# Multi-query attention: where the row maxima join the stacked queries

## The reference, cut to what matters

```
q = (x @ Wq + bq).reshape(Bx, Tx, HEADS, HD)
k = (x @ Wk + bk)[:, :, None, :]
att = jnp.einsum('bthd,bThd->bhtT', q, k) / math.sqrt(HD)
att = jnp.where(causal, -jnp.inf, att)
att = jax.nn.softmax(att, axis=-1)
```

## Time and profile before

| | us |
|---|---|
| median of 3 runs | 1833.64 (1832.84 to 1834.93) |
| the profiled execution, whole | 1835.51 |
| its span from first to last instruction | 1833.4 |

### The profile page before, as it was taken

How to read it: one execution, slowest core, us unless ns; L and a number is a source line. 1 busy time by engine, 2 the same in 40 slices (tenths; PEclk the granted TensorE clock), 3 DMA queues, 4 the chain that set the end, 5 groups by cost and what they waited for, 6 DMA issues and landing times. The chain is left out here.

```text
span 1833.4 us, 25467 instructions
## 1 busy us (share of the span) xinstructions
PE 1655.7 (90%) x7232; PEld 1261.5 (69%) x7232; DVE 1175.8 (64%) x1999; ACT 1196.7 (65%) x2231; POOL 1274.3 (70%) x1025
## 2 busy tenths in 40 slices
PE   3688989889898979898699999997999999999998
PEld 2355766767676757686366666664788888888887
DVE  5668677686959586564466666662556665665655
ACT  2236575756575655676277787885677777777776
POOL 3568597777878676667177777776567676767765
PEclk8788999999999999999699999998899999999999
DMA  3012222122121222332000000000233333333331
GB/s 116 1 46 58 64 62 65 59 62 71 57 71 58 69 58 75 94 98 63 1 1 1 1 2 0 1 1 18 75 94 102 98 93 103 98 98 96 100 93 52
DMA packets 115177, 108.96 MB, mean 59 GB/s; under 512 B 7003, under 2 KB 81888, under 8 KB 115040
## 3 DMA queue, kind: packets, MB, share of 16 engines
q1 hardware_dynamic: 115040, 107.39, 19.8%
HBM read 105.27 MB, written 2.10 MB: 59 GB/s over the span
## 5 line engine op out<-in xcount | busy, mean ns | idle before, releaser
L465 POOL TENSOR_TENSOR ARENA_R<-ARENA,ARENA_R 128x512 fp32r<-128x512 f32 x384 | 573.6, 1495 | 330.5 <-ACT ARENA_R L460 328.9
L557 DVE TENSOR_TENSOR ARENA<-ARENA,pair 128x512 f32<-128x512 f32 x512 | 350.0, 684 | 415.8 <-PE pair L340 330.4
L517 ACT ACTIVATE ARENA<-bank 128x512 f32<-128x512 f32 x512 | 305.0, 596 | 319.9 <-PE bank L340 319.2
L338 PE MATMUL pair<-ARENA_R 128*128 128x512 f32 x1064 | 423.2, 398 | 44.4 <-ACT ARENA L918 19.1
L339 PE MATMUL pair<-ARENA_R 128*128 128x512 f32 x1064 | 417.7, 393 | 0.0
L340 PE MATMUL pair<-ARENA_R 128*128 128x512 f32 x1064 | 417.4, 392 | 0.0
L527 ACT ACTIVATE ARENA_R<-ARENA 128x512 fp32r<-128x512 f32 x512 | 319.6, 624 | 57.8 <-DVE ARENA L557 57.4
L533 DVE TENSOR_TENSOR ARENA_R<-ARENA,ARENA_R 128x512 fp32r<-128x512 f32 x384 | 313.7, 817 | 0.0
L842 POOL TENSOR_TENSOR ARENA_R<-ARENA,ARENA_R 128x512 fp32r<-128x512 f32 x192 | 249.5, 1313 | 79.9 <-ACT ARENA L1026 76.4
L338 PEld LDWEIGHTS pair<-ARENA_R 128*128 128x128 f32 x1064 | 202.8, 191 | 104.0 <-ACT ARENA L918 22.5
L338 PE MATMUL bank<-ARENA_R 128*128 128x512 f32 x568 | 242.4, 427 | 19.2 <-DVE ARENA L1502 14.4
(11 more groups left out here) (213 smaller groups left out, 2252.4 us busy)
## 6 DMA issues: line engine op xcount, KB each, us to landing
ARENA<-in_L_ffn_Wg_dram SPq DMA_DIRECT2D x128, 256.0 KB, 2.6
ARENA<-in_L_ffn_Wu_dram SPq DMA_DIRECT2D x128, 256.0 KB, 2.6
ARENA<-in_L_ffn_Wd_dram SPq DMA_DIRECT2D x128, 256.0 KB, 2.8
X<-in_L_attn_a_x_dram SPq DMA_DIRECT2D x8, 256.0 KB, 5.7
out_dram<-X SPq DMA_DIRECT2D x8, 256.0 KB, 3.2
CST<-in_tables_dram SPq DMA_DIRECT2D x1, 835.5 KB, 5.0
ARENA<-in_tables_dram SPq DMA_DIRECT2D x1, 768.0 KB, 5.2
CST<-in_tables_dram SPq DMA_DIRECT2D x1, 256.0 KB, 4.9
```

The costliest lines, as they stand in the source:

```text
L338: pe.matmul(dst, wh, xh, start=start, stop=False)
L465: g.tensor_tensor(WL[:, x % 2, part, :], WS[:, x % 2, part, :], WH[:, x % 2, part, :].bitcast(F32), ALU.subtract).then_inc(F.wl, 1)
L517: act.activation(SG[:, c % 2, :], bank[c % 2], ACT.Silu).then_inc(F.sil, 1)
L557: v.tensor_tensor(HF[:, c % FC, :], SG[:, c % 2, :], bank[2 + c % 2], ALU.mult).then_inc(F.mul, 1)
```

## The change

The identity product of `stack2` goes: the two products with the maxima now start and end the group in PSUM by themselves. ScalarE's two copies go. VectorE gets `add_maxima`: for h = 0 and 1, one tensor_tensor that adds the stacked queries (from SBUF) to the bank (from PSUM) and writes Q2. It stands in VectorE's slot behind maximum k = 1. Waits that guarded QST by `q2_ready` now name `q2_used`, as VectorE reads QST.

```
@@ ScalarE
-                    if k == T_LAG - 1 and live(t, b, 1):
-                        o, ob = n - 1, 1 - b
-                        for h in range(2):
-                            act.wait_ge(B.q2_ready, 2 * o + h + 1)
-                            after(act, B.t_ready, UNITS * o)
-                            act.activation(Q2[:, 2 * h:2 * h + 2, :],
-                                           r3(bank[6 + h], 2), ACT.Copy).then_inc(B.q2_used, 1)
-                    after(act, B.q2_ready, 4 * (nxt.n - 1))
+                    after(act, B.q2_used, 4 * (nxt.n - 1))
@@ TensorE, stack2
-                    pe.matmul(dst, SELR[:, SID, :], QST[:, p, j, ob * SEQ:(ob + 1) * SEQ], start=True, stop=False)
                     for a in range(2):
                         m = pe.matmul(dst[:, a * P:(a + 1) * P], NMP[:, a, j, :], SELR[:, SID, :],
-                                      start=False, stop=(a == 1))
+                                      start=True, stop=True)
@@ VectorE
+            def add_maxima(o, p, ob):
+                for h in range(2):
+                    js = slice(2 * h, 2 * h + 2)
+                    v.wait_ge(B.q2_ready, 2 * o + h + 1)
+                    after(v, B.t_ready, UNITS * o)
+                    v.tensor_tensor(Q2[:, js, :], QST[:, p, js, ob * SEQ:(ob + 1) * SEQ].bitcast(F32),
+                                    r3(bank[6 + h], 2), ALU.add).then_inc(B.q2_used, 1)
...
                     if t.real():
                         maximum(t, b, k)
+                    if k == T_LAG - 1 and live(t, b, 1):
+                        add_maxima(n - 1, t.p if b == 1 else 1 - t.p, 1 - b)
```

More of the change, by code:

```diff
@@ L1009, in slot @@
                         if closing(t, b, k, (0, 8 + part)):
-                            act.wait_ge(B.q2_ready, 2 * NSEQ)
+                            act.wait_ge(B.q2_used, 2 * NSEQ)
                             hi_part(act, NE * NT, part)
@@ L1729, in slot @@
                     if closing(t, b, k, (0, 8)):
-                        v.wait_ge(B.q2_ready, 2 * NSEQ)
+                        v.wait_ge(B.q2_used, 2 * NSEQ)
                         f_lo(v, NT, bank[0])
```

## The result

| | median of its runs, us | ratio to the kernel before, 95% interval |
|---|---|---|
| before | 1834.45 (1832.84 to 1835.14) | |
| after | 1841.34 (1836.0 to 1843.22) | 1.0035 [1.0025, 1.0045] |

The change costs 6.9 us by the medians, 4.6 to 8.3 us by the interval of the ratio. The forecast was 1834.8 us and "the same", with 1829 to 1840 as its range; the measured time lies above it. The profiled execution took 1842.64 us, its span 1840.7 us.

The account below looks back on a forecast made before the run. TensorE was taken to set the pace, with the path through Q2 to `cols` deciding once its work shrinks. Terms -0.7 + 1.3 + 1.0 - 0.4 = +1.2 us on 1833.64 gave 1834.8 us, range 1829 to 1840.

Parts of the forecast that it names:

- TensorE's part: In stack2, each identity product costs TensorE's queue 0.115 us; four per slot 0.46 us, 7.4 us over 16 slots.
- The addition: VectorE's new operation after stack2 takes 0.69 us, two take 1.34 us; starts at P + 0.87 with VectorE free.
- The second rival: GpSimd stretches VectorE's additions from 685 to 817 ns: 4.2 us slower in all, 1839 us; chance 0.12.
- P to `cols`: From stack2's first product (P) to `cols`, which needs Q2: 2.35 us with VectorE free, 2.47 to 2.55 busy.
- The last slot: Slot before the experts: GpSimd's low parts and the experts' normalisation begin earlier, gaining 0.4 us, bounds 0 and 1.18.
- the mechanism that was named: In the last slot, ScalarE's exponentials no longer wait behind its copies, so GpSimd's low parts and the experts' normalisation start earlier.
- Behind the branch: One slot behind the loop's branch: VectorE starts its maxima at 1074.67, additions follow late, `cols` loses 1.0 us.
- The third rival: VectorE's longer program brings another late start ahead of an addition, 1 to 3 us each: 1837 to 1840 us; chance 0.06.
- The first rival: The saving on TensorE comes through, up to 7.4 us gained over 16 slots: 1826 us; chance 0.09.

Follow-up runs that it names:

- e2: The changed kernel with the loop of tiles 2 to 5 written out on all engines; 1833.99 us, ratio 0.9997.
- e1: The kernel before with the loop of tiles 2 to 5 written out on all engines; 1831.95 us, ratio 0.999.
- e6: e2 with the four identity products put back as overwritten filler in the first stack2 alone; 1829.86 us, ratio 0.9978.
- e7: The kernel before with six already met waits more in each of VectorE's slots, behind maximum k = 1; 1835.38 us, ratio 1.0007.
- e5: e4 (half of the change) with the loop of tiles 2 to 5 written out; 1828.43 us, ratio 0.9967.
- e9: e5 with the two missing identity products of h = 0 as filler in the first stack2 alone; 1828.75 us, ratio 0.9972.
- e3: The changed kernel with the four identity products of each stack2 put back as overwritten filler; 1838.15 us, ratio 1.0022.
- e10: e8, loop kept, with the filler products of e6 in the first stack2; 1834.31 us, ratio 1.0003.
- e8: The changed kernel without the two waits on t_ready in add_maxima, which TensorE's order implies; 1836.6 us, ratio 1.0009.
- e4: Half of the change: bank h = 0 by VectorE's addition, h = 1 by identity product and ScalarE's copy as before; 1832.85 us, ratio 0.9999.

## Why the prediction was wrong, point by point

- **TensorE's part** was right. Eight products without the identities run from P = 1105.35 to the next line at 1106.29 in after, 0.117 us each; 0.115 was said. The 81 ns of the Trainium skill (page "TensorE: Matmul & The Clock Gate", section "Back-to-back issue gap") are not reached in this kernel without the 256-column products either.
- **The addition** was right: 671 to 689 ns in 32 cases (0.69 said), 1.28 us for two instead of 1.34. It started at P + 0.78 or 0.88 where VectorE was free (0.87 said). The second rival (GpSimd stretches them to 0.82 us) fell, as the Trainium skill's rule on VectorE instructions with one SBUF input has it (page "SBUF — State Buffer", section "Who interferes with whom").
- **P to `cols`** came out a little shorter than said: with VectorE free 2.12 to 2.33 us (2.35 said), with VectorE busy 2.39 (2.47 and 2.55 said). The starting point was off too: the prediction took the 2.45 us of one slot for all seven with VectorE free, but four of them have 2.35 in the kernel before. So the seven gained 0.13 us (three) and 0.22 (four) where 0.1 was said, and the busy ones lost 0.04 and 0.12 where 0.12 and 0.28 were said. With the clock at its upper level and no branch, 14 slots from the second P to the last take 303.51 us in e2 and 305.39 in e1, a gain of 1.9 us. Eight of these have VectorE free and six busy, two of them of the later kind; by the prediction's terms that is a loss of 0.2.
- **The last slot** gained 0.97 us in after, 0.4 said, within its bounds. By the mechanism that was named it gained 0.56: the experts' normalisation (line 421) starts at P + 8.49 instead of P + 9.05. The rest is no more than two executions of the same last slot differ by (41.38 us in before and 42.04 in e1; 40.52 in e2 and 41.10 in e6).
- **Behind the branch** the step failed. It took 1074.67, the time at which VectorE came back in the kernel before, for a constant. The third rival had the right thought, that VectorE's longer program may bring more of this standstill, but as one more gap elsewhere, at 0.06. It was the same gap, 2.3 us longer, and its row gave reason to suspect it: idle for 2.91 us in front of the maxima k = 0 and 1, where the usual slot with b = 0 has 0.38 us in front of k = 0 (below, timeline of before) and 1.04 in front of k = 1. e7 shows it without any addition. With that gap the loss of 1.0 us became 5.43: 3.00 us of idleness of TensorE, and 2.43 us more of work, at the lower clock.

```profile
1026.96 0.69 DVE L1628 TENSOR_REDUCE ARENA<-bank 128x4 f32<-128x512 f32 x1 [0.38 <-PE bank L1235]
```

- **The clock** had no term in the sum at all, and that is the larger of the two steps that made the prediction wrong. "At full granted clock" was read as a property of the stage. It was a property of the kernel's order. The prediction said that 0.36 us of the saved work "turns into a wait", and priced a wait at its length. In the first slot TensorE already waited 1.7 us ahead of stack2, where a usual slot has 0.5 us; there a wait of 0.77 us for the additions, where the kernel before waited 0.17 for ScalarE's copies (below), came with a loss of 4.45 us, 3.94 of it slower work. The two events are 9.9 us of the table above, of which the longer busy time makes 6.4 and TensorE's idleness 3.5; the rest of the slots gained 2.1 us and the start 0.4.

```profile
920.31 0.49 PE L1256 MATMUL pair<-ARENA_R 128*128 128x512 f32 x1 [0.17 <-ACT ARENA_R L996]
```

- The first rival's price, 1826 us, is near the lowest times of e2 (1826.75) and e6 (1826.66). That doesn't speak for the rival: the loop's cost is gone there too, and the medians are 1833.99 and 1829.86.

## What to carry to other kernels

Before taking work off TensorE, find the places where it already waits longest, and ask what the granted clock does if the saved work becomes waiting too; one such place can cost more than all the others save, and whether it does can differ from one execution to the next, so it takes many executions to see. Behind a loop's branch an engine that waits for no data may be late by microseconds that change with the length of its program, so put nothing on that engine's path there, or write the loop out when its passes are few. When a step is limited by one engine's latency, splitting it between two idle engines (e5, e9) may bring what moving it whole does not: 0.47 us per two slots against 0.23.

## What the runs showed of the hardware that was not expected

- Four products of 0.115 us in the first stack2, with `cols` at the same distance from P, go with a first slot of 20.40 us (e3, e6, e10); without them it took 25.19 to 25.21 us (after, e2, e8). It isn't certain in each execution: the profile of e4, with ten products, has no fall (20.48 us) where that of e5, with the same ten, has one (24.84).
- After the fall the clock stayed at 1.2 GHz for 10.2 us in the first slot and 6.9 us behind the branch. In both stretches TensorE was again busy almost throughout (4.93 of 5.00 us, 6.61 of 7.00 us).
- Behind the branch TensorE's wait and the fall don't go together simply, one profile each: none after 1.36 us (e7) and 2.33 us (e8), one of 3.4 us after 2.15 us (e10), one of 6.9 us that begins in a wait of 2.06 us (after).
- VectorE's standstill in front of the maxima behind the branch has two sizes in seven profiles: 2.87 to 2.91 us (before, e4, e8, e10) and 4.96 to 5.32 us (after, e3, e7). Where it is short and an addition follows (e4, e8, e10), VectorE stands another 0.90 to 1.08 us in front of the addition.
